# Cross-attention in fp32: the product with V moved ahead of the output projection in every step of TensorE and ScalarE

## The reference

```python
q   = heads(x @ to_q_w)                       # x: (32, 512, 640)
k,v = heads(ctx @ to_k_w), heads(ctx @ to_v_w)  # ctx: (32, 77, 1024)
p   = softmax(einsum('bhqd,bhkd->bhqk', q, k) / sqrt(32))
out = merge(einsum('bhqk,bhkd->bhqd', p, v)) @ to_out_w + to_out_b + x
```

## Time and profile before

| | |
|---|---|
| median of 3 runs | 1845.51 us (1843.35 to 1846.19) |
| the profiled execution's own time | 1846.19 us |
| its span, first to last instruction | 1844.5 us |
| TensorE, busy share of the span | 97% |
| VectorE, ScalarE, GpSimd | 63%, 57%, 37% |
| mean granted TensorE clock | 0.989 of full speed |

### The profile page before, as it was taken

One profiled execution on the slowest core, in us unless ns is written; L12 is line 12 of the kernel. 1 busy time (PEld: TensorE's weight loads), 2 busy tenths in 40 slices (PEclk: granted clock), 3 DMA queues, 4 the chain that ended last, 5 costly groups with the idle time before them and its releaser, 6 DMA issues.

```text
span 1844.5 us, 41902 instructions
## 1 busy us (share of the span) xinstructions
PE 1796.0 (97%) x14960; PEld 1508.3 (82%) x14960; DVE 1167.8 (63%) x2402; ACT 1054.0 (57%) x5597; POOL 689.8 (37%) x865
## 2 busy tenths in 40 slices
PE   8999998689999999999999999999999999999997
PEld 7999998468888888888888888888888888888886
DVE  3201010577777777777777777777777777777762
ACT  4312111476666666666666666666666666666661
POOL 1111111244444444444444444444444444444441
PEclk9999999799999999999999999999999999999998
DMA  7422110588989989989898998988989989998973
GB/s 264 136 85 86 63 44 33 143 227 250 252 247 247 252 249 250 249 250 252 246 251 251 249 250 247 253 248 248 250 251 249 250 249 251 246 254 246 253 217 125
DMA packets 271397, 399.36 MB, mean 217 GB/s; under 512 B 41088, under 2 KB 119024, under 8 KB 271200
## 3 DMA queue, kind: packets, MB, share of 16 engines
q1 hardware_dynamic: 183008, 301.62, 56.1%
q10 hardware_dynamic: 83904, 82.59, 18.5%
q0 software_dynamic: 4288, 12.62, 1.9%
HBM read 216.37 MB, written 180.39 MB: 215 GB/s over the span
## 4 chain that ended last, share of the span: by engine, by line
PE 78%; DVE 1%; ACT 1%; DMA 0%; POOL 0%; issue 0%; SPq 0%; ACTq 0%; DVEq 0%
PE p_bank L735 31%; PE p_bank L776 31%; PE p_scores L750 9%; PE p_bank L762 8%; ACT probs L595 1%; DVE negmax L638 0%; POOL probs L562 0%; DMA probs_t<-p_scratch 0%; DVE turned L654 0%; DMA p_scratch<-turned 0%; DVE x_raw L671 0%; DVE x_t L676 0%; DVE q_t L661 0%; DVE rsum L644 0%; DVE x_bias L684 0%
## 5 line engine op out<-in xcount | busy, mean ns | idle before, releaser
L595 ACT ACTIVATE probs<-p_scores,negmax 128x77 f32<-128x77 f32 x2560 | 787.8, 361 | 332.0 <-DVE negmax L638 332.0
L562 POOL TENSOR_TENSOR probs<-probs,rsum 128x308 f32<-128x308 f32 x640 | 446.5, 700 | 844.4 <-DVE rsum L644 844.3
L595 ACT ACTIVATION_READ_ACCUMULATOR probs<-p_scores,negmax 128x1 f32 x2560 | 622.1, 243 | 0.0
L735 PE MATMUL p_bank<-x_t,wq_split 128*128 128x512 f32 x2400 | 598.9, 401 | 15.8 <-DVE x_t L676 15.8
L776 PE MATMUL p_bank<-wo_split,o_t 128*128 128x320 f32 x3840 | 599.4, 310 | 0.6 <-DVE x_bias L684 0.6
L776 PEld LDWEIGHTS p_bank<-wo_split,o_t 128*128 128x128 f32 x3840 | 578.4, 189 | 17.4 <-issue 2.5
L735 PEld LDWEIGHTS p_bank<-x_t,wq_split 128*128 128x128 f32 x2400 | 445.1, 190 | 116.8 <-DVE x_t L676 17.0
L654 DVE STREAM_TRANSPOSE turned<-probs 128x384 f32<-128x384 f32 x640 | 356.8, 558 | 29.3 <-POOL probs L562 29.0
L638 DVE TENSOR_REDUCE negmax<-p_scores 128x16 f32<-128x1232 f32 x160 | 227.7, 1423 | 86.4 <-PE p_scores L750 86.4
L750 PEld LDWEIGHTS p_scores<-k_sb,q_t 32*128 32x128 f32 x5120 | 157.5, 186 | 146.9 <-issue 146.9
L644 DVE RECIPROCAL rsum<-sums 128x4 f32<-128x4 f32 x640 | 111.1, 174 | 187.6 <-ACT probs L595 183.3
(11 more groups left out here) (28 smaller groups left out, 634.2 us busy)
## 6 DMA issues: line engine op xcount, KB each, us to landing
p_scratch<-turned SPq DMA_DIRECT2D x160, 768.0 KB, 6.8
probs_t<-p_scratch SPq DMA_DIRECT2D x320, 256.0 KB
x_bias<-in_x ACTq DMA_DIRECT2D x128, 320.0 KB, 3.5
out<-x_bias SPq DMA_DIRECT2D x128, 320.0 KB, 5.6
x_raw<-in_x ACTq DMA_DIRECT2D x124, 320.0 KB, 5.5
probs_t<-p_scratch SPq DMA_DIRECT2D x160, 104.0 KB
ctx_raw<-in_ctx SPq DMA_DIRECT2D x19, 512.0 KB, 4.6
k_sb<-k_scratch SPq DMA_DIRECT2D x32, 192.5 KB, 6.1
```

Of the source, the lines that this page charges most:

```text
L562: nc.gpsimd.tensor_tensor(heads_of(t), heads_of(t), rsum[:, slot, t, :].unsqueeze(2).to_broadcast([P, HG, N_TXT]), ALU.mult).then_inc(prob ...
L595: last = nc.scalar.activation(heads_of(t)[:, h, :], s_bank[:, h, t * N_TXT:(t + 1) * N_TXT], ACT.Exp, bias=negmax[:, slot, t, h:h + 1], ac ...
L735: last = nc.tensor.matmul(q_bank[:, :], wq_s[:, w, c, g * P:(g + 1) * P], x_t[:, a, c, :], start=c == 0 and i == 0, stop=c == CC - 1 and i ...
```

## The change

V is taken ahead of the fill (and, on ScalarE, ahead of the DMA issues and of the rounding of x) in every step. Nothing is added or left out; only the order within the step differs. In step 4, O3 keeps its place ahead of Q.

```diff
-TENSOR = orders("S Q0 Q1 Q2 Q3 Q4 P5 V",
-                "S Q0 Q1 Q2 Q3 Q4 P6 P7 V",
-                "S Q0 Q1 Q2 Q3 Q4 O0 V",
-                "S Q0 Q1 Q2 Q3 Q4 O1 O2 V",
-                "S O3 Q0 Q1 Q2 Q3 Q4 O4 V")
-SCALAR = orders("S0 S1 S2 S3 D1 V",
-                "S0 S1 S2 S3 D2 D3 V",
-                "S0 S1 S2 S3 R0 V",
-                "S0 S1 S2 S3 R1 R2 X0 X1 X2 X3 X4 V",
-                "S0 S1 S2 S3 R3 E0 V")
+TENSOR = orders("S Q0 Q1 Q2 Q3 Q4 V P5",
+                "S Q0 Q1 Q2 Q3 Q4 V P6 P7",
+                "S Q0 Q1 Q2 Q3 Q4 V O0",
+                "S Q0 Q1 Q2 Q3 Q4 V O1 O2",
+                "S O3 Q0 Q1 Q2 Q3 Q4 V O4")
+SCALAR = orders("S0 S1 S2 S3 V D1",
+                "S0 S1 S2 S3 V D2 D3",
+                "S0 S1 S2 S3 V R0",
+                "S0 S1 S2 S3 V R1 R2 X0 X1 X2 X3 X4",
+                "S0 S1 S2 S3 V R3 E0")
```

## The result

The changed kernel takes 1900.92 us (median of 4 runs, 1899.89 to 1902.59) against 1845.85 us for the kernel before in the same runs. The ratio is 1.0299, with a 95% interval of 1.0281 to 1.0317. The forecast was 1902.5. The profiled execution took 1897.36 us, its span is 1895.7 us: 51.2 us more than that of before. By the medians the change costs 55.1 us.

The account below looks back on a forecast made before the run. TensorE, busy without any wait in the steady part, was taken as the bound. 1846.2 + 30.6 (extra changes of kind) + 26.4 (V's waits) = 1903.2, stated as 1902.5 us because the median lies 0.7 lower; range 1872 to 1940.

Parts of the forecast that it names:

- The change of kind: On TensorE, a fill directly behind V adds one switch of tile kind, 0.20 us for each of 153 fills, 30.6 us.
- loads run ahead: Rival: the fill's weights load under V's last matmuls, the new switch is free, V's waits cost 38 us: 1884 us; 8%.
- the faster rival: Rival: S's loads run under the fill's last matmuls, so S shrinks by half a microsecond: 1826 us; 3%.
- V comes before its data: In steps 1, 2 and 3, the earlier V waits for its reads of the probabilities: 0.88 us a batch, 26.4 us.
- the 90 pieces forecast: TensorE's list of waits would show V's read waits, some 26 us in about 90 pieces, in steps 1, 2 and 3.
- my 6.0: Assumed time in us from a read's first issue until V starts; mean of two V at the end, bounds 5.55 and 7.41.
- step 2 would live on step 1's wait: Step 1's wait of 0.32 us wins back lead for step 2, whose V then waits only 0.16 us.
- What costs nothing: ScalarE's V wait goes, DMA issues and rounding of x fall behind one activation of 0.6 us: no cost.
- The clock: TensorE's clock stays at full speed; the rival that V's waits halve it once a batch said 1993 us, 4%.
- The additions on VectorE: In steps 0 and 2 the fill's addition ahead of T3 ends later, but 0.39 us of cover hides it: no cost.
- V's other wait: V's wait for W to empty `pv_bank` in the same step; Q covers it with 1.3 us to spare in step 1.

Follow-up runs that it names:

- experiment 6: Kernel before with TensorE's V between the two fills in steps 1 and 3, ahead in 0 and 4, behind in 2; ScalarE as before: 1870.92 us, ratio 1.0135.
- experiment 3: Kernel before with V ahead of the fill in steps 0 and 4 only, on both engines: 1859.84 us, ratio 1.0071.
- experiment 5: Kernel before with TensorE's V between the two fills in steps 1 and 3, ahead of the fill in the others; ScalarE as before: 1879.13 us, ratio 1.0180.
- tight_steps: Kernel before with V ahead of the fill in steps 1, 2 and 3 only, on both engines: 1893.86 us, ratio 1.0253.
- experiment 1: Kernel before with only TensorE's order changed, V ahead of the fill in all five steps; ScalarE as before: 1892.22 us, ratio 1.0260.
- experiment 7: The changed kernel run once more, without further edit: 1899.02 us, ratio 1.0292 against the kernel before.
- experiment 11: Changed kernel with ScalarE's step 3 as before, V behind its two loads and the rounding of x: 1890.49 us, ratio 1.0243 against the kernel before.
- experiment 9: Kernel before with ScalarE's V ahead of the DMA issues in steps 0, 1, 2 and 4; TensorE as before: 1980.83 us, ratio 1.0708.

## Why the prediction was right, and where its terms were off

**The change of kind: 153 x 0.20 = 30.6 us.** Right in mechanism and size. The traces have 2.39 to 2.40 for a fill behind V, experiment 6 gives 24.6 us for 122, and experiment 3 gives 14 us for 61, whose interval (10.7 to 15.7) holds 12.2. The rival "loads run ahead" falls: without a wait of V the kernel would have stayed at 1846 in experiment 6. S behind a fill was neither dearer nor cheaper, 1.06, so the faster rival falls too.

**V comes before its data: 26.4 us.** The mechanism is right: moving V by half the fills in steps 1 and 3 (experiment 5) takes the waits away and leaves the changes of kind. The size is off, and so is the picture behind it. The idle time in front of V grew from 7.1 to 26.9 us, so 19.8 us; 1.1 of it only moved there in batch 1, from in front of S. But of the 90 pieces forecast there are 28 in the steady part, with 15.7 us: 13 in step 1, 14 in step 3, one in step 2.

The batch I read was not the reason. Over all steady batches of the kernel before, the leads are 5.24, 5.69 and 4.74 us in the middle for steps 1, 2 and 3, close to the 5.28, 5.12 and 4.72 of that one batch, though single ones run from 3.6 to 9.5 in step 3. Nor were the reads short: where V of the changed kernel waited for them, it started 5.2 to 7.8 us after their issue, 6.5 in the middle, against my 6.0. What failed is that I let the reads' issue stand still. Counted from S of their own step, SyncE issued the reads for V of steps 1, 2 and 3 17.33, 16.91 and 17.86 us later in the kernel before, and 16.21, 16.22 and 17.51 us later in the changed one (middle values of 26 batches). So 1.1, 0.7 and 0.35 us of lead came from a part of the chain, mostly the write's issue and its landing, that I had taken as fixed, and mostly V was not late. They are earlier in experiment 6 too, where no V waits (16.66, 16.54, 17.48). The DMA engines are less full in both (0.86 and 0.88 against 0.90), which fits; what makes it so was not tried.

That step 2 would live on step 1's wait was not seen: V of step 2 waited in one batch, though step 1 had no wait to give in half of them. That the lead lost and won between S and V of a step counts fits `tight_steps`: with fewer changes of kind, V waits more.

**What costs nothing: ScalarE's order.** This step failed. I wrote that D, E, R and X fall behind one activation of 0.6 us. In the full change ScalarE's order costs 7 to 9 us (experiments 1, 7, 11), all through V's waits, and it comes from step 3. So the two errors hide each other: with TensorE's order alone the idle time in front of V grows by 10.6 us (17.7 against 7.1), less than half of what I forecast, and ScalarE's order brings it back up. A forecast of 1902.5 for 1900.92 owes part of its closeness to that, which is luck. The sum itself was 57.0 us, for the profiled execution, where the spans differ by 51.2 us; the medians differ by 55.1.

**The clock.** It stays at full speed in the steady part, as said. At the start of batch 1 it falls for a moment, but in the kernel before too, one group earlier. TensorE's timelines there, before and after:

```profile
395.50 1.13 PE L750 MATMUL p_scores<-k_sb,q_t 32*128 32x77 f32 x32 [1.64 <-ACT probs L595]
396.56 5.30 PE L735 MATMUL p_bank<-x_t,wq_split 128*128 128x512 f32 x15
401.70 2.36 PE L776 MATMUL p_bank<-wo_split,o_t 128*128 128x320 f32 x15
```

```profile
396.67 3.69 PE L735 MATMUL p_bank<-x_t,wq_split 128*128 128x512 f32 x15
403.78 1.69 PE L762 MATMUL p_bank<-probs_t,v_sb 77*32 77x512 f32 x8 [3.42 <-DMA probs_t<-p_scratch]
405.40 3.41 PE L776 MATMUL p_bank<-wo_split,o_t 128*128 128x320 f32 x15
408.74 1.13 PE L750 MATMUL p_scores<-k_sb,q_t 32*128 32x77 f32 x32
```

In the changed kernel V waited 3.42 us, and then V and the fill took 0.6 and 1.0 us longer than at full speed. In the kernel before, Q took 5.14 us from start to start instead of 3.54, so 1.6 us as well. The clock therefore adds nothing to the difference between the two kernels.

The pages close without it: TensorE is busy for 1828.4 - 1796.0 = 32.4 us more and idle for 18.8 us more, 51.2 in all. Of the busy time 30.6 us are the changes of kind. The remaining 2 us fit a V that comes late by less than 0.15 us, which the lists don't count as a wait: from Q's start to V's it is mostly 3.71 us in steps 1 and 3, and 3.64 in steps 0 and 2.

**The additions on VectorE** were covered, as said: in the steady part no row of TensorE waits for VectorE. Only at the very end does V's other wait show, the one for W: V(158), behind the last step, waits 3.45 us for it, in the place of the 4.80 us for reads the earlier trace rows.

## What to carry to other kernels

On a TensorE that never idles, order isn't free: count how often the kind of tile changes in a step, because at each change the weight loads stand idle until the old kind is through, here 0.20 us by 153. A consumer of a long DMA chain belongs as late as its own consumers allow; look for where the engine does idle, as at the end here, and put ready work there. A wait put into a queue ahead of DMA issues delays the DMAs, even when the waiting instruction's engine has nothing else to do, and the price can be many times that of the wait itself, the more so when the idle time that it causes on TensorE brings the clock down.

## What the runs showed that was not expected

- The same edit on ScalarE costs 7 to 9 us or some 150 us, depending on whether TensorE's V comes early or late. An idle engine's wait is harmless only if nothing is queued behind it that somebody needs: waits at V like the one of 2.45 us, once in a step, became 168.2 us of waiting for x on VectorE, and in experiment 9 some 60 us of the price are S and Q at half speed.
- Writing 6% fewer bytes (374.53 instead of 399.36 MB in all) in five DMAs instead of one made the kernel 6 us slower; issuing four DMAs of 26 KB took 1.7 to 3.8 us, 2.6 in the middle.
- The length of one wait did not say whether the clock falls. Behind 3.42 us in front of V it fell, and behind 2.53 us in front of S in experiment 9, but also behind 1.64 us in front of S in the kernel before, where waits of 2.08 and 0.47 us stood a little earlier; waits of up to 1.8 us in the steady part of the changed kernel never lowered it, nor did one of 2.61 us in experiment 9.
